# A decoder layer on one core: the product with values of each attention unit, split into two halves of 256 queries with score tiles between them

## The chip, the cores and the metric

One core of one Trainium2 chip. The metric is the device time of one launch in microseconds; three runs of a kernel are made and the median counts. TensorE (PE), VectorE (DVE), ScalarE (ACT), GpSimd (POOL) and SyncE (SP) each run their own instruction list in order and wait on semaphores that the others raise.

## What is computed

A decoder layer with two attentions and a feed-forward part, each behind a layer norm and added to its input. x is 4 x 1024 x 256 in float32, 16 heads of 16 columns.

```python
x = x + _L0_attn_ref(_layernorm(x), W_qkv, b_qkv, W_out, b_out)
x = x + _L0_xattn_ref(_layernorm(x), ctx_1024, ctx_1024, Wq, bq, Wk, bk, Wv, bv, Wo, bo)
x = x + _L0_ffn_ref(_layernorm(x), W_fc, ln_w, ln_b, W_proj)
...
energy = jnp.einsum('bqhe,bkhe->bqhk', q, k)            # attention over 1024 keys
attn = jax.nn.softmax(energy, axis=-1) / sqrt(E)
out = jnp.einsum('bihv,bvhd->bihd', attn, v)
```

The change lies in the first attention alone: 4 batches x 16 heads x 1024 queries x 1024 keys.

## The kernel before

The kernel has three stages: projections to queries, keys and values (about the first 130 us), the attention over 1024 keys (to about 785 us), and cross attention with the feed-forward part (the rest). The change touches the second.

**Units.** The heads are taken in groups of four, so there are 16 groups of a batch and four heads. A group has two halves of 512 queries, and each half has eight blocks of 128 keys. One *unit* U (0 to 255) is one block of keys against one half of the queries for the four heads. `KB` is 8, `CH` is 512, `UNITS` is 16. For each unit TensorE does three kinds of work.

- `scores(U, k)` (L1543), k = 0 to 3: the transposed score tile of one head, 128 keys by 512 queries, in float32r. It goes to one of three PSUM banks in turn, so tile n waits until the exponential of tile n - 3 is done (`exp_done`).
- `values(U)` (L1556): four matmuls with 32 columns of values each, side by side in the four column groups of the array, in float32. They read the probabilities of the unit and add up in bank 4 over the eight units of a half. It waits until all four exponentials of the unit are done. The last unit's matmul stops the sum, ScalarE copies bank 4 to `ot`, and the first unit of the next half waits for that (`o_copied`).
- `max_tile(t)` (L1427): a score tile with the queries on the partitions, one of 32 for each half of a later group, from which VectorE takes the row maxima that the softmax subtracts. There are four for each unit. They go round four banks (3, 5, 6, 7), so one waits for VectorE's reduction of the tile four places earlier (`max_reduced`). The maxima are split in two parts, transposed by TensorE (`max_transpose`, L1527, once for every 32 tiles, ahead of the tile with t % 32 == 8), copied by ScalarE to `mt` (L711), and written by SP into the rows of the queries that the score tiles read (`m_loaded`).

A score tile contracts over 50 rows and a maximum tile over 48, in one of two strips of 64 partitions (0 to 63, or 64 to 127), by the head. Two neighbours on different strips run at once.

**Order.** It is written out by hand for each engine. TensorE's loop over U is the one the diff shows: a maximum tile, a score tile of the next unit, three times over, then the product with values, then the next unit's fourth score tile and the fourth maximum tile. After `LAST_ROWS` (243) there are no more maximum tiles and other work of the next stage comes in. ScalarE's order is

```python
            for U in range(GROUPS * UNITS):
                if U % KB == 4 and U // KB + 1 < HALVES - 1:
                    m_copy(U // KB + 1)
...
                if U + 1 < GROUPS * UNITS:
                    act.wait_ge(pv_done, U)
                    exps(U + 1, 0, 3)
...
                if U % KB == KB - 1:
                    act.wait_ge(pv_done, U + 1)
                    act.wait_ge(o_written, O_WRITES * (U // KB))
                    act.activation(ot[:], ps[:, 4, :], ACT.Copy).then_inc(o_copied, 1)
                if U + 1 < GROUPS * UNITS:
                    exps(U + 1, 3, 4)
```

The probabilities have two buffers, so the exponentials of unit U + 1 wait for the product of unit U - 1 (`pv_done`). `m_copy` waits for the transpose (`m_transposed`). In units 72, 74, 76 and 78 ScalarE also takes the absolute values of a piece of the feed-forward weights (L729). VectorE reduces the maximum tiles one after another (L1021).

Of the kernel before, what the change touches and what calls it, by code (L numbers as in the profile page):

```python
# [30 lines left out]
CH = 512  # L31
NCH = T // CH
# [8 lines left out]
GROUPS = B * NG  # L41
KB = S // P
QC = S // CH
UNITS = QC * KB
# [52 lines left out]
EARLY_TILES = 2 * EARLY_PAIRS * (NCH - EARLY)  # L97
LEAD = EARLY_TILES
LAST_ROWS = GROUPS * UNITS - 13
# [19 lines left out]
HALVES = 2 * GROUPS  # L119
# [32 lines left out]
def build(nc, x, ctxT, wqkv, bqk, bv, wout, bout, wqT, bq2, wkT, bk2, wvT, bv2, woT, bo2,  # L152
# [10 lines left out]
    with ctx:  # L163
        def sb(name, shape, dt=F32, where=ctx):
            return where.enter_context(nc.sbuf_tensor(name, shape, dt))
# [4 lines left out]
        ps = ctx.enter_context(nc.psum_tensor("ps", [P, 8, 512], F32))  # L170
# [48 lines left out]
        prob = sb("prob", [P, 2, 2, 2, CH], F32, ab)  # L219
        Qs = [sb(f"Qs{i}", [P, HG // STRIPS, S], F32, ab) for i in range(NG)]  # L220
        Ks = [sb(f"Ks{i}", [P, HG // STRIPS, S], F32, ab) for i in range(NG)]
        V_all = sb("V_all", [P, V_ALL + D], F32, ab)
# [65 lines left out]
        parts_ready = sem("parts_ready")  # L288
# [6 lines left out]
        max_reduced = sem("max_reduced")  # L295
# [7 lines left out]
        pv_done = sem("pv_done")  # L303
# [1082 lines left out]
        def _(pe):  # L1386
# [125 lines left out]
            def max_tile(t):  # L1512

                if t >= TILES:
                    return
                if t % HALF == 8:
                    max_transpose(t // HALF - 1)
                if t % MAXT == 0:
                    b, g = divmod(t // MAXT, NG)
                    pe.wait_ge(group_loaded[g], GROUP_LOADS * (b + (g > 0)))  # L1520
                score_tile(max_bank("tile", t), t)

            def max_transpose(f):

                r = max_bank("rows", f)
                pe.wait_ge(m_split, f + 1)
                pe.transpose(ps[:, r, 0:P], msp[:], ident[:]).then_inc(m_transposed, 1)  # L1527

            def scores(U, k):

                group, s = divmod(U, UNITS)
                if group == NG * B:
                    return
                g, (qc, kb) = group % NG, divmod(s, KB)
                n, j = 4 * U + k, ST_HEADS[k]
                if kb == 0 and k == 0:
                    pe.wait_ge(m_loaded, 16 * HG * (U // KB + 1))
                if n in ST_BEFORE:
                    pe.wait_ge(exp_done, ST_BEFORE[n] + 1)
                elif n >= ST_TAIL:  # L1540
                    pe.wait_ge(max_reduced, TILES)
                    pe.wait_ge(m_copied, HALVES)
                pe.matmul(ps[:, ST_BANK[n], :], stack(Ks[g], j, ROWS, slice(kb * P, (kb + 1) * P)),  # L1543
                          stack(Qs[g], j, ROWS, slice(qc * CH, (qc + 1) * CH)), start=True, stop=True).then_inc(st_done, 1)

            def values(U):

                group, s = divmod(U, UNITS)
                b, g = divmod(group, NG)
                kb = s % KB  # L1550
                pe.wait_ge(exp_done, 4 * U + 4)
                if kb == 0 and U:
                    pe.wait_ge(o_copied, U // KB)
                for j in range(HG):
                    v = ((b * KB + kb) * H + g * HG + j) * VCOL
                    i = pe.matmul(ps[32 * j:32 * j + 32, 4, :], V_all[:, v:v + 32],  # L1556
                                  prob[:, U % 2, j // 2, j % 2, :], start=(kb == 0), stop=(kb == KB - 1))
                i.then_inc(pv_done, 1)

            freed = {"t2": (t2_copied, 2), "q2": (q2_copied, 2), "s": (less_done, 8), "pt": (pt_copied, 8), "val": (o2_copied, 2),  # L1560
                     "o2": (x2_added, 2), "out": (x1_added, 2), "t3": (t3_low, 2)}
# [49 lines left out]
            def q2(c, m):  # L1611
                if not 0 <= c < NCH:
                    return
                pe.wait_ge(t2_copied, 2 * c + 2)
                r = x_bank("q2", c, m)
                for k in range(KT):
                    n = mm(ps[:, r, :], w_q2[:, k, m * P:(m + 1) * P], xn2T[:, k, :], k, KT)
                n.then_inc(q2_done, 1)
# [2 lines left out]
            scores(0, 3)  # L1621
            for U in range(GROUPS * UNITS):
                t = LEAD + 4 * U
                if U == LAST_ROWS:
                    max_transpose(HALVES - 1)
                max_tile(t)
                scores(U + 1, 0)
                max_tile(t + 1)
                scores(U + 1, 1)
                if U == 0:  # L1630
                    pe.wait_ge(max_reduced, EARLY_TILES)
                max_tile(t + 2)
                scores(U + 1, 2)
                if U == 0:
                    pe.wait_ge(parts_ready, 4 * NCH)
                if U > LAST_ROWS:
                    scores(U + 1, 3)
                if U == GROUPS * UNITS - 1:
                    q2(0, 0)
                values(U)  # L1640
                if LAST_ROWS < U <= LAST_ROWS + 3:
                    prepare(U - LAST_ROWS - 1)
                if TAIL_OUT <= U < TAIL_OUT + 2:
                    out_proj(0, U - TAIL_OUT)
                if U == TAIL_T2:
                    t2(0, 0)
                    t2(0, 1)
                if U <= LAST_ROWS:
                    scores(U + 1, 3)
                max_tile(t + 3)  # L1650


            pe.wait_ge(exp_done, EXPS)
            def x_scores(c, t):
# [229 lines left out]
```

## Time and profile before

| | |
|---|---|
| median of three runs | 1169.06 us (1167.9 to 1171.06) |
| the profiled execution | 1169.54 us, its span 1167.6 us |
| PE busy | 1133.1 us, 97% |
| DVE busy | 992.8 us, 85% |
| ACT busy | 856.8 us, 73% |
| attention stage, 130 to 785 us | PE 651.54, DVE 616.33, ACT 535.53 us busy of 655.00 |
| granted TensorE clock in that stage | 1.00 |

The busy time of PE counts the time in which a matmul is anywhere between its start and its modelled end, so two starts may lie further apart than the work needs and PE still reads as busy. What an engine needs is read from starts that follow one another without a wait. A timeline row merges neighbours of one kind: its first number is the start of the first, its second the time from there to the end of the last, and xN is their count. A float32 matmul makes two records of weight load and matmul (so the product with values of a unit is x8), a float32r one makes one.

### The profile page before, as it was taken

How to read it: one execution, taken by the hardware profiler on the slowest of the kernel's cores; microseconds unless marked ns; L12 is line 12 of the kernel's file. 1: busy time of each engine (PE TensorE's matmuls, PEld its weight loads, DVE VectorE, ACT ScalarE, POOL GpSimd, SP SyncE). 2: the span in 40 equal slices, each digit the busy share in tenths (PEclk: the TensorE clock that was granted, in tenths of full speed). 3: DMA queues.
4: the chain of work that ended last, by engine and by line, in shares of the span. 5: the costliest groups of instructions: out<-in, count | busy, mean ns of one | idle time of the engine just before them, and what ended most of it. 6: DMA issues, size and time to landing. Idle time of an engine off the chain costs nothing.

```text
span 1167.6 us, 19014 instructions
## 1 busy us (share of the span) xinstructions
PE 1133.1 (97%) x6664; PEld 597.5 (51%) x6664; DVE 992.8 (85%) x1863; ACT 856.8 (73%) x1606; POOL 303.9 (26%) x469
## 2 busy tenths in 40 slices
PE   8999999999999999999999999999899999999986
PEld 6544333333333333333333333344568778778776
DVE  5678899999999999999999999976768778878844
ACT  4312588888888888888888888876468877788874
POOL 2124010220220220220121000012665656565532
PEclk9999999999999999999999999999899999999998
DMA  5878113562321330340341300023301220200001
GB/s 180 267 217 234 75 21 51 112 138 31 62 47 23 65 60 7 66 60 14 58 61 33 45 7 11 7 67 83 89 26 33 76 70 4 73 19 19 1 19 37
DMA packets 45918, 74.98 MB, mean 64 GB/s; under 512 B 10112, under 2 KB 23808, under 8 KB 45824
## 3 DMA queue, kind: packets, MB, share of 16 engines
q1 hardware_dynamic: 36176, 46.50, 13.7%
q0 software_dynamic: 9648, 27.27, 13.6%
q8 instruction: 53, 0.87, 0.3%
q14 instruction: 41, 0.34, 0.1%
HBM read 47.53 MB, written 25.69 MB: 63 GB/s over the span
## 4 chain that ended last, share of the span: by engine, by line
PE 88%; DVE 5%; ACT 4%; issue 1%; DMA 1%; SPq 1%; POOL 0%; DVEq 0%; ACTq 0%; POOLq 0%
PE ps L1543 22%; PE ps L1556 22%; PE ps L1388 18%; PE ps L1427 10%; PE ps L1746 5%; PE ps L1664 2%; PE ps L1733 2%; PE ps L1676 2%; ACT ot L781 1%; ACT prob L718 1%; PE ps L1687 1%; PE ps L1593 1%; DVE maxes L1014 1%; DMA Ks<-qk_scratch 1%; PE ps L1527 1%
## 5 line engine op out<-in xcount | busy, mean ns | idle before, releaser
L1021 DVE TENSOR_REDUCE maxes<-ps 128x1 f32<-128x512 f32 x968 | 606.8, 683 | 31.7 <-PE ps L1427 15.4
L718 ACT ACTIVATE prob<-ps 128x512 f32<-128x512 f32 x1024 | 531.8, 603 | 119.2 <-PE ps L1543 117.7
L1543 PE MATMUL ps<-Qs,Ks 50*128 50x512 f32 x1024 | 377.0, 452 | 4.3 <-ACT prob L718 2.0
L1543 PEld LDWEIGHTS ps<-Qs,Ks 50*128 50x128 f32 x1024 | 168.3, 185 | 309.8 <-ACT prob L718 298.3
L1427 PE MATMUL ps<-Ks,Qs 48*128 48x512 f32 x1024 | 322.1, 432 | 3.0 <-DVE maxes L1014 2.6
L1556 PE MATMUL ps<-prob,V_all 128*32 128x512 f32 x2048 | 273.6, 606 | 0.0
L1427 PEld LDWEIGHTS ps<-Ks,Qs 48*128 48x128 f32 x1024 | 166.8, 186 | 50.5 <-DVE maxes L1014 15.9
L378 POOL DMA_DIRECT2D Qs<-qk_scratch x90 | 44.5, 502 | 466.5 <-PE ps L1556 466.3
L606 POOL TENSOR_TENSOR pe_<-pe_,rsum 128x512 f32<-128x512 f32 x64 | 68.4, 1076 | 78.1 <-DVE rsum L1232 78.1
L1746 PE MATMUL ps<-t_p,fT 128*128 128x256 f32 x512 | 77.1, 297 | 2.4 <-DVE fT L1271 2.4
L1204 DVE TENSOR_REDUCE nmx<-ps 128x8 f32<-128x512 f32 x64 | 43.6, 681 | 39.9 <-PE ps L1664 39.9
L1556 PEld LDWEIGHTS ps<-prob,V_all 128*32 128x32 f32 x2048 | 40.3, 108 | 63.6 <-ACT prob L718 43.6
L1746 PEld LDWEIGHTS ps<-t_p,fT 128*128 128x128 f32 x512 | 66.8, 191 | 11.0 <-issue 7.3
L705 ACT ACTIVATE parts<-ps,b_qk 128x512 fp32r<-128x512 f32 x32 | 22.0, 688 | 68.0 <-PE ps L1388 68.0
L1388 PE MATMUL ps<-t_fc,xn3T 128*128 128x512 f32 x256 | 68.3, 409 | 0.2 <-DVE xn3T L1263 0.2
L1271 DVE SCALAR_TENSOR_TENSOR fT<-ps,ln_w,fT 128x512 fp32r<-128x512 f32 x64 | 46.9, 740 | 19.3 <-ACT fT L885 19.2
L1388 PE MATMUL ps<-xnT_a,w_qkv 128*128 128x512 f32 x128 | 61.3, 612 | 0.0
L885 ACT ACTIVATE fT<-ps,ln_w 128x512 fp32r<-128x512 f32 x64 | 43.5, 687 | 21.7 <-PE ps L1733 20.2
L1388 PEld LDWEIGHTS ps<-t_fc,xn3T 128*128 128x128 f32 x256 | 46.3, 188 | 14.5 <-issue 5.7
L562 POOL TENSOR_TENSOR x_b<-x_in,b_out 128x1024 f32<-128x1024 f32 x8 | 18.9, 2362 | 128.9 <-DMA x_in<-in_x 128.9
L806 ACT ACTIVATE pT<-ps 128x512 f32<-128x512 f32 x64 | 36.5, 595 | 21.3 <-PE ps L1676 21.2
L1223 DVE TENSOR_REDUCE psum<-pe_ 128x8 f32<-128x512 f32 x64 | 42.7, 668 | 6.9 <-ACT pe_ L797 6.7
(153 smaller groups left out, 1276.2 us busy)
## 6 DMA issues: line engine op xcount, KB each, us to landing
qk_scratch<-parts SPq DMA_DIRECT2D x32, 512.0 KB, 5.2
Qs<-qk_scratch POOLq DMA_DIRECT2D x90, 128.0 KB, 5.2
Ks<-qk_scratch POOLq DMA_DIRECT2D x90, 128.0 KB, 7.5
o_scratch<-ot SPq DMA_DIRECT2D x128, 32.0 KB
x_in<-in_x SPq DMA_DIRECT2D x8, 512.0 KB, 7.0
on_raw<-o_scratch SPq DMA_DIRECT2D x8, 512.0 KB
r_raw<-r_scratch SPq DMA_DIRECT2D x16, 256.0 KB
out<-xo SPq DMA_DIRECT2D x8, 512.0 KB, 2.9
```

Source lines behind the costliest of these rows:

```text
L378: queue.dma_start(dst[lo:lo + D, :, :], heads[r]).then_inc(loaded[g], 16)
L606: pool.tensor_tensor(p, p, rsum[:, i, :, None].broadcast_to([P, 8, CTX]), ALU.mult).then_inc(p_ready, 1)
L718: act.activation(prob[:, U % 2, j // 2, j % 2, :], ps[:, ST_BANK[n], :], ACT.Exp).then_inc(exp_done, 1)
L885: act.activation(fT[:, place, 0, :].bitcast(F32R), ps[:, r, :], ACT.Identity, scale=ln_w[:, t:t + 1]).then_inc(fh_ready, 1)
L1021: dve.tensor_reduce(maxes[:, qc, j * BLK + blk, half:half + 1], ps[:, MAX_BANK["tile", t], :], AX.X, ALU.max).then_inc(max_reduced, 1)
L1204: dve.tensor_reduce(nmx[:, i, :], ps[:, BANK["s", c, i], :].rearrange("p (h t) -> p h t", h=8), AX.X, ALU.max, negate=True).then_inc(nmx_d ...
L1271: dve.scalar_tensor_tensor(out=fT[:, place, 1, :].bitcast(F32R), in0=ps[:, r, :], scalar=ln_w[:, t:t + 1], in1=fT[:, place, 0, :], op0=ALU ...
L1388: return pe.matmul(o, lhsT, rhs, start=(k == 0), stop=(k == n - 1), **kw)
L1427: pe.matmul(ps[:, bank, :], stack(Qs[g], j, STACK, slice(q0, q0 + P)), stack(Ks[g], j, STACK, slice(half * 512, (half + 1) * 512)), start= ...
L1543: pe.matmul(ps[:, ST_BANK[n], :], stack(Ks[g], j, ROWS, slice(kb * P, (kb + 1) * P)), stack(Qs[g], j, ROWS, slice(qc * CH, (qc + 1) * CH)) ...
L1556: i = pe.matmul(ps[32 * j:32 * j + 32, 4, :], V_all[:, v:v + 32], prob[:, U % 2, j // 2, j % 2, :], start=(kb == 0), stop=(kb == KB - 1))
L1746: i = pe.matmul(ps[:, 6 + blk // 2, (blk % 2) * E:(blk % 2 + 1) * E], fT[:, ft_bank(c, t)[1], part, blk * P:(blk + 1) * P].bitcast(F32R), ...
```

## The change

TensorE's order in the units up to 243, and the shape of the product with values. The product of a unit is done in two halves, queries 0 to 255 and 256 to 511, each of four matmuls; only the unit that ends a half of the queries (U % 8 == 7) keeps it whole. Between the halves stand three of the four maximum tiles, score tiles 2 and 3 of the next unit, and score tile 0 of the unit after that; behind the second half stand the fourth maximum tile and score tile 1 of the unit after next. The sum in bank 4 starts with the first half of the first unit and ends with the second half of the last. No other engine's order changes.

```diff
-            def values(U):
+            def values(U, lo=0, hi=CH):
...
-                if kb == 0 and U:
+                if kb == 0 and lo == 0 and U:
                     pe.wait_ge(o_copied, U // KB)
                 for j in range(HG):
                     v = ((b * KB + kb) * H + g * HG + j) * VCOL
-                    i = pe.matmul(ps[32 * j:32 * j + 32, 4, :], V_all[:, v:v + 32],
-                                  prob[:, U % 2, j // 2, j % 2, :], start=(kb == 0), stop=(kb == KB - 1))
-                i.then_inc(pv_done, 1)
+                    i = pe.matmul(ps[32 * j:32 * j + 32, 4, lo:hi], V_all[:, v:v + 32], prob[:, U % 2, j // 2, j % 2, lo:hi],
+                                  start=(kb == 0 and lo == 0), stop=(kb == KB - 1 and hi == CH), skip_group_check=True)
+                if hi == CH:
+                    i.then_inc(pv_done, 1)
...
-                if U == LAST_ROWS:
-                    max_transpose(HALVES - 1)
-                max_tile(t)
-                scores(U + 1, 0)
-                max_tile(t + 1)
-                scores(U + 1, 1)
-                if U == 0:
-                    pe.wait_ge(max_reduced, EARLY_TILES)
-                max_tile(t + 2)
-                scores(U + 1, 2)
...
-                values(U)
+                if U <= LAST_ROWS:
...
+                    if U % KB == KB - 1:
+                        values(U)
+                    else:
+                        values(U, 0, CH // 2)
+                    if U:
+                        max_tile(t)
+                        max_tile(t + 1)
+                        max_tile(t + 2)
+                    scores(U + 1, 2)
+                    scores(U + 1, 3)
+                    scores(U + 2, 0)
+                    if U % KB < KB - 1:
+                        values(U, CH // 2, CH)
+                    max_tile(t + 3)
+                    scores(U + 2, 1)
+                else:
+                    for k in range(2 if U == LAST_ROWS + 1 else 0, 4):
+                        scores(U + 1, k)
+                    if U == GROUPS * UNITS - 1:
+                        q2(0, 0)
+                    values(U)
...
-                if U <= LAST_ROWS:
-                    scores(U + 1, 3)
-                max_tile(t + 3)
```

TensorE, units 3 and 4 before: the end of unit 3 (its product is the x3 row of line 1556), then unit 4, which has the transpose of the maxima. L1543 is a score tile, L1427 a maximum tile, L1556 values, L1527 the transpose.

```order
L1556 MATMUL ps<-prob,V_all 32x512 x3
L1543 MATMUL ps<-Qs0,Ks0 128x512 [waits exp_done]
L1427 MATMUL ps<-Ks1,Qs1 128x512 [waits max_reduced]
L1527 MATMUL ps<-ident,msp 128x128 [waits m_split,max_reduced]
L1427 MATMUL ps<-Ks1,Qs1 128x512 [waits max_reduced]
L1543 MATMUL ps<-Qs0,Ks0 128x512 [waits exp_done]
L1427 MATMUL ps<-Ks1,Qs1 128x512 [waits max_reduced]
L1543 MATMUL ps<-Qs0,Ks0 128x512 [waits exp_done]
L1427 MATMUL ps<-Ks1,Qs1 128x512 [waits max_reduced]
L1543 MATMUL ps<-Qs0,Ks0 128x512 [waits exp_done]
L1556 MATMUL ps<-prob,V_all 32x512 [waits exp_done]
L1556 MATMUL ps<-prob,V_all 32x512 x3
```

The same place now, from the end of unit 3 (last pair) to unit 4's second half and last pair.

```order
L1543 MATMUL ps<-Qs0,Ks0 128x512 [waits exp_done]
L1556 MATMUL ps<-prob,V_all 32x256 [waits exp_done]
L1556 MATMUL ps<-prob,V_all 32x256 x3
L1527 MATMUL ps<-ident,msp 128x128 [waits m_split,max_reduced]
L1427 MATMUL ps<-Ks1,Qs1 128x512 [waits max_reduced] x3
L1543 MATMUL ps<-Qs0,Ks0 128x512 [waits exp_done] x3
L1556 MATMUL ps<-prob,V_all 32x256 [waits exp_done]
L1556 MATMUL ps<-prob,V_all 32x256 x3
L1427 MATMUL ps<-Ks1,Qs1 128x512 [waits m_copied]
L1543 MATMUL ps<-Qs0,Ks0 128x512 [waits exp_done]
```

The transpose stood ahead of the whole product and now stands behind its first half. The three score tiles in the middle are tiles 2 and 3 of unit 5 and tile 0 of unit 6. An ordinary unit is the same without the transpose.

TensorE at unit 7, the last of its half, and the start of unit 8 now.

```order
L1556 MATMUL ps<-prob,V_all 32x512 [waits exp_done]
L1556 MATMUL ps<-prob,V_all 32x512 x3
L1427 MATMUL ps<-Ks1,Qs1 128x512 [waits max_reduced] x3
L1543 MATMUL ps<-Qs0,Ks0 128x512 [waits exp_done] x3
L1427 MATMUL ps<-Ks1,Qs1 128x512 [waits max_reduced]
L1543 MATMUL ps<-Qs0,Ks0 128x512 [waits exp_done]
L1556 MATMUL ps<-prob,V_all 32x256 [waits o_copied,exp_done]
L1556 MATMUL ps<-prob,V_all 32x256 x3
```

The whole product is followed by all eight tiles; before, three score tiles of the next unit stood ahead of it and the fourth behind.

## Rows read from the trace of the kernel before

**Rows 1.** The page: busy time by engine; the group of VectorE's reductions.

```profile
PE 1133.1 (97%) x6664; PEld 597.5 (51%) x6664; DVE 992.8 (85%) x1863; ACT 856.8 (73%) x1606; POOL 303.9 (26%) x469
...
L1021 DVE TENSOR_REDUCE maxes<-ps 128x1 f32<-128x512 f32 x968 | 606.8, 683 | 31.7 <-PE ps L1427 15.4
```

**Rows 2.** Waits, 300 to 700 us: who waited for whom, us, times, longest.

```profile
PEld ps L1543 <- ACT prob L718: 183.5, 290, 1.0
ACT prob L718 <- PE ps L1543: 66.7, 129, 0.6
```

**Rows 3.** Timeline, two ordinary units: start us, us, engine, line, operation.

```profile
609.24 1.06 PE L1556 MATMUL ps<-prob,V_all 128*32 128x512 f32 x8
...
612.84 0.49 PE L1543 MATMUL ps<-Qs,Ks 50*128 50x512 f32 x1
...
613.18 0.62 PE L1543 MATMUL ps<-Qs,Ks 50*128 50x512 f32 x2
...
613.37 2.07 ACT L718 ACTIVATE prob<-ps 128x512 f32<-128x512 f32 x4 [0.54 <-PE ps L1543]
...
613.42 0.61 PE L1427 MATMUL ps<-Ks,Qs 48*128 48x512 f32 x2
...
614.02 0.50 PE L1543 MATMUL ps<-Qs,Ks 50*128 50x512 f32 x1
...
614.45 1.06 PE L1556 MATMUL ps<-prob,V_all 128*32 128x512 f32 x8
```

**Rows 4.** Timeline, the unit that ends a half.

```profile
615.45 0.50 PE L1543 MATMUL ps<-Qs,Ks 50*128 50x512 f32 x1
...
615.58 0.60 ACT L781 ACTIVATE ot<-ps 128x512 f32<-128x512 f32 x1
...
616.08 2.06 ACT L718 ACTIVATE prob<-ps 128x512 f32<-128x512 f32 x4
...
617.15 1.06 PE L1556 MATMUL ps<-prob,V_all 128*32 128x512 f32 x8
```

**Rows 5.** Timeline, PE, near the stage's end: streamed score tiles, then a product.

```profile
782.30 0.73 PE L1543 MATMUL ps<-Qs,Ks 50*128 50x512 f32 x4
782.96 1.06 PE L1556 MATMUL ps<-prob,V_all 128*32 128x512 f32 x8
```

**Rows 6.** Timeline, DVE, 608.9 to 610.1 us.

```profile
608.80 1.87 DVE L1021 TENSOR_REDUCE maxes<-ps 128x1 f32<-128x512 f32 x3
```

**Rows 7.** Timeline, the unit with the transpose of the maxima.

```profile
603.89 1.07 PE L1556 MATMUL ps<-prob,V_all 128*32 128x512 f32 x8
...
605.32 0.33 PE L1527 MATMUL ps<-ident,msp 128*128 128x128 f32 x1
...
605.91 0.25 ACT L711 ACTIVATE mt<-ps 32x128 fp32r<-32x128 f32 x1
...
606.21 1.57 ACT L718 ACTIVATE prob<-ps 128x512 f32<-128x512 f32 x3
...
606.63 1.07 PE L1556 MATMUL ps<-prob,V_all 128*32 128x512 f32 x8
```

**Rows 8.** Groups by form, 0 to 170 us: float32 matmuls; busy us, mean ns.

```profile
L1388 PE MATMUL ps<-xnT_a,w_qkv 128*128 128x512 f32 x128 | 61.3, 612 | 0.0
L1388 PE MATMUL ps<-w_qkv,xnT_a 128*128 128x256 f32 x128 | 31.7, 391 | 4.6 <-DMA Ks<-qk_scratch 3.4 <-ACT xnT_a L699 0.8 <-ACT mt L711 0.4
```

**Rows 9.** Timelines of ACT and PE, a unit with an absolute-value pass.

```profile
319.97 1.06 ACT L729 ACTIVATE kbd<-w_fc 128x1024 f32<-128x1024 f32 x1
...
321.01 3.52 ACT L718 ACTIVATE prob<-ps 128x512 f32<-128x512 f32 x7
...
320.56 1.07 PE L1556 MATMUL ps<-prob,V_all 128*32 128x512 f32 x8
...
323.54 1.05 PE L1556 MATMUL ps<-prob,V_all 128*32 128x512 f32 x5
```

**Rows 10.** Timeline, PE, last stage: transposes in a stream.

```profile
1099.07 1.04 PE L1593 MATMUL ps<-ident,xn 128*128 128x128 f32 x8
```

More of the change, by code:

```diff
@@ L1623, in _ @@
                 t = LEAD + 4 * U
-                if U == LAST_ROWS:
-                    max_transpose(HALVES - 1)
-                max_tile(t)
-                scores(U + 1, 0)
-                max_tile(t + 1)
-                scores(U + 1, 1)
-                if U == 0:
-                    pe.wait_ge(max_reduced, EARLY_TILES)
-                max_tile(t + 2)
-                scores(U + 1, 2)
-                if U == 0:
-                    pe.wait_ge(parts_ready, 4 * NCH)
-                if U > LAST_ROWS:
-                    scores(U + 1, 3)
-                if U == GROUPS * UNITS - 1:
-                    q2(0, 0)
-                values(U)
+                if U <= LAST_ROWS:
+                    if U == LAST_ROWS:
+                        max_transpose(HALVES - 1)
+                    if U == 0:
+                        max_tile(t)
+                        scores(1, 0)
+                        max_tile(t + 1)
+                        scores(1, 1)
+                        pe.wait_ge(max_reduced, EARLY_TILES)
+                        max_tile(t + 2)
+                        pe.wait_ge(parts_ready, 4 * NCH)
+                    if U % KB == KB - 1:
[3 more added lines that the diff above has]
+                    if U:
+                        max_tile(t)
+                        max_tile(t + 1)
+                        max_tile(t + 2)
+                    scores(U + 1, 2)
+                    scores(U + 1, 3)
+                    scores(U + 2, 0)
[9 more added lines that the diff above has]
+                    values(U)
                 if LAST_ROWS < U <= LAST_ROWS + 3:
```

## The prediction

> **What bounds the kernel now.** I read the page first, then the stage in question by its waits, then one stretch of it instruction by instruction. The page says PE 97% busy [rows 1], which reads like a TensorE bound. The view of waits over 300 to 700 us corrects this [rows 2]: TensorE's weight loads for score tiles wait 183.5 us for ScalarE's exponentials, and ScalarE waits 66.7 us for score tiles. Two engines that both wait for each other form a loop, and the timeline gives its links [rows 3]. A unit begins where its product with values starts (609.24, two units later 614.45: 2.605 us each). The last score tile of the next unit follows it (612.84), its exponential starts 0.53 us later (613.37), a score tile that reuses the bank starts 0.65 us after that (614.02), the next product 0.43 us later (614.45), and it holds TensorE for 1.00 us (to 615.45 [rows 4]). 0.53 + 0.65 + 0.43 + 1.00 = 2.61: the whole period is this chain. TensorE's own work is less. From 612.84 the pairs of tiles on opposite row strips start 0.34 and then 0.24 us apart (613.18, 613.42); 1.00 + 0.34 + 0.24 + 0.24 and 0.33 from a streamed pair into a product (782.30 + 0.73 - 0.39 = 782.64 to 782.96 [rows 5]) give 2.15, so 0.46 us of each unit is stall. VectorE needs 4 reductions; one lasts 0.68 us and the next starts (1.87 - 0.68) / 2 = 0.60 us after it [rows 1, 6], so 2.40. ScalarE needs 4 exponentials of (2.07 - 0.60) / 3 = 0.49 us [rows 3], 1.95.
>
> Two units in every eight are longer. The one that ends a half of the queries has ScalarE's copy to ot between its exponentials: 614.45 to 617.15, 2.70 us [rows 3, 4]. The one with the transpose of the maxima has the copy to mt in front of them: 603.89 to 606.63, 2.74 us [rows 7]. So eight units take 6 x 2.605 + 2.70 + 2.74 = 21.07 us.
>
> **The change in an ordinary unit.** Call the start of the first half of the product 0. The product is two passes of four matmuls in each of which columns set the length; 512 against 256 columns in float32 differ by 612 - 391 = 221 ns [rows 8], so each pass is about 0.22 us shorter and a half takes 1.00 - 0.44 = 0.56 us. The bounds of this: 0.50 (exactly half of 1.00), and 0.70 if the fixed part were kept twice and each switch cost another 0.1. Then TensorE runs three pairs: two maximum tiles at 0.56, a maximum tile with score tile 2 at 0.90, score tile 3 with tile 0 of the unit after at 1.14. The second half starts at 1.47, the last pair at 2.03, and the next first half 0.43 later (a pair fresh after a product, as 614.02 to 614.45): **2.46 us** of own work, 0.31 more than the 2.15 of before. The added cost is the second entry and exit of the product.
>
> The Trainium skill (TensorEngine Tiling (Array Packing), Key Properties) says that changing the tiling mode drains TensorE, which speaks against a change that doubles these switches. The trace agrees: 0.33 us into a product against 0.24 between pairs.
>
> The chain of waits is now another: score tile 2 starts at 0.90, its exponential 0.44 later (a streamed tile's record is 0.1 shorter than the 0.5 of a fresh one, so 0.53 less 0.09), the fourth exponential 0.485 after it, and 0.65 later it releases the next first half: 0.56 + 0.34 + 0.44 + 0.485 + 0.65 = **2.475 us**. It is just over TensorE's 2.46 and over VectorE's 2.40, so 2.475 is the period and 0.13 us a unit is gained. The cover is thin: three limits lie within 0.08 us. The score tiles in the middle don't stall: tile 0 of unit U+2 (1.14) waits for the second exponential, which starts at 0.32 and releases it at 0.97.
>
> **The unit with the transpose.** Before, the transpose stood ahead of the product and ScalarE's copy to mt was ready when ScalarE came to it: 605.32, copied at 605.91, next exponential at 606.21, 0.30 later [rows 7]. Now it stands behind the first half, which itself waits for the fourth exponential. ScalarE's order is unchanged: right behind that exponential it waits for the transpose. So: transpose at 0.56, copy at 0.56 + 0.33 + 0.03 = 0.92, first exponential of the next unit at 1.22 where an ordinary unit has it at -0.165, the second at 1.705. Tile 0 of unit U+2 needs the second: 1.705 + 0.65 = 2.355. It is in front of the second half in TensorE's order, which starts at 2.785; the last pair at 3.345, the next product at 3.345 + 0.43 = **3.775 us**, against 2.74 before. Queued behind the stalled tile are the second half, a maximum tile and a score tile; VectorE loses nothing that counts, since it has over a microsecond to spare in this unit.
>
> **The unit that ends a half.** Its product stays whole, but score tiles 2 and 3 of the next unit now come behind it; before, tile 2 came ahead, so that its exponential ran under the product. ScalarE's copy to ot stands between the exponentials of tiles 2 and 3. Chain: product 1.00, a pair 0.34, to the exponential 0.44, to the copy 0.485, to the fourth exponential 616.08 - 615.58 = 0.50, release 0.65 = **3.41 us**, against 2.70 before.
>
> **The rest.** Eight units: 6 x 2.475 + 3.775 + 3.41 = 22.04 us, 0.97 more than 21.07. There are 30 such eights in the 244 units that the change reorders (+29.0), and 4 ordinary units over (-0.5). In four units ScalarE also takes an absolute-value pass, which shifts the exponentials by 321.01 - 319.97 = 1.04 us; before, such a unit took 323.54 - 320.56 = 2.98, 0.375 over an ordinary one [rows 9]. By the same chain it takes now (0.875 for the first exponential, 2.01 for tile 0, 2.44 for the second half, 3.00, 3.43) 0.955 over one: +2.3. The m rows for the next half have from the copy at 605.91 + 0.25 to the first score tile that reads them some 7.0 us now and 3.775 + 2.475 + 1.14 - 1.17 = 6.2 after; no wait on them shows before, and I cost this at nothing. If their loads took longer than 6.2, each half would lose the excess. What comes before and behind the 244 units keeps its order and costs nothing. POOL's loads and SP's writes keep their place. Sum: +29.0 - 0.5 + 2.3 = **+30.8 us**. The profiled execution took 1169.54 us (0.5 over the median of the three, 1169.06): 1169.5 + 30.8 = **1200 us**, 2.6% slower.
>
> With a half at 0.50 an ordinary unit takes 2.415 and the transposing one 3.655: 21.56 for eight, 1187 us. With 0.70 TensorE's own work sets 2.46 + 2 x 0.14 = 2.74: 23.9 for eight, 1255 us; I take the low value since [rows 8] measure the difference itself.
>
> **Rivals.**
> (1) The copies don't hold. If ScalarE's two copies cost the new order no more than the old one, eight units take 6 x 2.475 + 2.70 + 2.74 = 20.29, which is 0.78 less: 1169.5 - 23.4 + 2 = 1148 us, **faster**. It decides at the point where the two long units together take less than 21.07 - 14.85 = 6.22 us; I get 7.19. For it: VectorE's four banks hold work over a short gap, and the normal unit is quicker. Against: VectorE is not what the chain waits for, and both copies stand in a strictly ordered queue between exponentials [rows 4, 7]. Chance 0.06.
> (2) TensorE can't issue fast enough. A float32 product is two records for each matmul, so a unit goes from 16 to 24 pairs of weight load and matmul. The densest long stream in the trace is transposes, (1.04 - 0.27) / 7 = 0.11 us each [rows 10]; 24 x 0.11 = 2.64 us a unit. That gives 6 x 0.165 x 30 = 30 us more: 1230 us. For: no stretch of the trace goes faster for long. Against: those transposes each load 128 columns of weights, values load 32. Chance 0.10.
> The Trainium skill (TensorE: Matmul & The Clock Gate, Wait — 56ns, not 53.3ns?) puts the sequencer at about 62 ns for a matmul without hardware decode; 24 of these would be 1.5 us, no bound, unless the loads cost as much again (an estimate of 3.0 us). No run here shows which.
> (3) The two effects cancel: the ordinary unit at 2.40 and the long ones 0.3 us shorter than worked out give 21.0 for eight, no change. Chance 0.04.
>
> **How the numbers follow.** My forecast, 1200, has 0.80. Within 0.3% (3.5 us, about what a measurement of this kernel can tell from no change) lies rival 3, 0.04. Faster is rival 1, 0.06. Slower is the rest, 0.90. The range leaves out rival 1 and the highest part of rival 2 and of the long half: low end the half at 0.50 less 0.2 us in the two long units of each eight, 1187 - 6 = 1181; high end 1230.
>
> **What would show it.** Starts of products in the profile after: ordinary units 2.4 to 2.5 apart, one of eight 3.8 with ScalarE idle ahead of the mt copy (a wait for the transpose, about 1.1 us, absent before), one of eight 3.4 with ScalarE idle ahead of the third exponential. A half should take 0.56 us, and the weight loads of score tiles should wait less for ScalarE in ordinary units. I am wrong if ScalarE doesn't wait for the transpose, or if ordinary units take over 2.6 us (rival 2 or a dearer half, told apart by whether the gap stands inside the products or between them).

## The result, and the profile after

| | before | changed |
|---|---|---|
| median of four runs | 1169.42 us | 1211.16 us (1204.31 to 1222.83) |
| ratio to before | | 1.034, 95% interval 1.029 to 1.038 |
| the profiled execution | 1169.54 us | 1211.86 us, span 1209.9 us |

3.4% slower, where 2.6% (1200 us) was forecast. Ratios here and below leave out executions over 1.5% above the fastest of their kernel; with a single core these are the ones in which TensorE's clock stayed low longest, of which more below.

The page of the changed kernel, with the lines that answer to [rows 1], ScalarE's exponentials and the granted clock (tenths of full speed, 40 slices of the span):

```profile
PE 1156.3 (96%) x8376; PEld 620.2 (51%) x8376; DVE 994.2 (82%) x1863; ACT 857.0 (71%) x1606; POOL 303.9 (25%) x469
...
PEclk9999999999959999999999999999999999999998
...
L1021 DVE TENSOR_REDUCE maxes<-ps 128x1 f32<-128x512 f32 x968 | 608.7, 683 | 74.2 <-PE ps L1427 70.7
L718 ACT ACTIVATE prob<-ps 128x512 f32<-128x512 f32 x1024 | 534.5, 599 | 134.9 <-PE ps L1543 125.1
```

VectorE and ScalarE do the same work as before (994 and 857 us), in a span 42 us longer. VectorE's idle time ahead of its reductions went from 31.7 to 74.2 us: it is starved more than before. TensorE again reads 96% busy, which says as little as before. The 5 in the clock's row is new.

The view of waits of the changed kernel, 410 to 810 us, as long a window as that of [rows 2] (columns as there):

```profile
PEld ps L1427 <- DVE maxes L1021: 84.4, 194, 0.8
...
PEld ps L1556 <- ACT prob L718: 49.1, 144, 0.8
...
PEld ps L1543 <- ACT prob L718: 22.5, 54, 0.7
ACT mt L711 <- PE ps L1527: 17.8, 18, 1.0
```

A line of the view of [rows 2] that answers to the first of these:

```profile
PEld ps L1427 <- DVE maxes L1021: 6.1, 19, 0.3
```

Score tiles wait far less for exponentials (22.5 us in 400 instead of 183.5), products wait more (49.1 us instead of 27.0), and ScalarE's copy to mt now waits for the transpose, 1.0 us each time. That wait was absent before. The line that grew most, TensorE's weight loads waiting for VectorE (6.1 to 84.4 us), is not what it seems. Most of it is the weight loader's idle time behind a half of a product, 0.41 us each time:

```profile
438.15 0.64 PE L1556 MATMUL ps<-prob,V_all 128*32 128x256 f32 x8
438.72 0.32 PEld L1427 LDWEIGHTS ps<-Ks,Qs 48*128 48x128 f32 x3 [0.41 <-issue]
...
439.63 0.64 PE L1556 MATMUL ps<-prob,V_all 128*32 128x256 f32 x8
440.20 0.18 PEld L1427 LDWEIGHTS ps<-Ks,Qs 48*128 48x128 f32 x1 [0.41 <-DVE maxes L1021]
```

The next tile comes 0.57 us after the start of the half in both places, whether the view names VectorE or nobody, so VectorE costs nothing there.

Timeline of the changed kernel, the unit with the transpose and the ordinary one behind it (columns as in [rows 7]):

```profile
440.66 0.64 PE L1556 MATMUL ps<-prob,V_all 128*32 128x256 f32 x8
441.23 0.33 PE L1527 MATMUL ps<-ident,msp 128*128 128x128 f32 x1
...
441.60 0.27 ACT L711 ACTIVATE mt<-ps 32x128 fp32r<-32x128 f32 x1 [0.99 <-PE ps L1527]
441.78 2.01 ACT L718 ACTIVATE prob<-ps 128x512 f32<-128x512 f32 x4
...
442.88 0.18 PEld L1543 LDWEIGHTS ps<-Qs,Ks 50*128 50x128 f32 x1 [0.30 <-ACT prob L718]
443.31 0.64 PE L1556 MATMUL ps<-prob,V_all 128*32 128x256 f32 x8
...
444.31 0.64 PE L1556 MATMUL ps<-prob,V_all 128*32 128x256 f32 x8
444.88 0.73 PE L1427 MATMUL ps<-Ks,Qs 48*128 48x512 f32 x3
445.22 0.63 PE L1543 MATMUL ps<-Qs,Ks 50*128 50x512 f32 x3
445.78 0.64 PE L1556 MATMUL ps<-prob,V_all 128*32 128x256 f32 x8
...
446.81 0.64 PE L1556 MATMUL ps<-prob,V_all 128*32 128x256 f32 x8
```

Counted from 440.66: transpose at 0.57, copy at 0.94 after ScalarE had idled 0.99, the third score tile (tile 0 of the unit after next) only at 2.22, second half at 2.65, next product at 3.65. The ordinary unit: 444.31 to 446.81, 2.50 us; a half is followed by the next tile after 0.57 us.

And the unit that ends a half, whole product and all tiles behind it (compare [rows 4]):

```profile
449.33 1.06 PE L1556 MATMUL ps<-prob,V_all 128*32 128x512 f32 x8
...
451.13 0.60 ACT L718 ACTIVATE prob<-ps 128x512 f32<-128x512 f32 x1 [0.87 <-PE ps L1543]
451.62 0.59 ACT L781 ACTIVATE ot<-ps 128x512 f32<-128x512 f32 x1
...
452.10 1.58 ACT L718 ACTIVATE prob<-ps 128x512 f32<-128x512 f32 x3
452.75 0.16 PEld L1556 LDWEIGHTS ps<-prob,V_all 128*32 128x32 f32 x8 [0.79 <-ACT prob L718]
```

3.42 us from product to product, with ScalarE idle 0.87 us for tile 2. (This whole product is also what ends the sum in bank 4, not a second half.) Eight units take 6 x 2.505 + 3.64 + 3.42 = 22.09 us; read from the starts of the products, 26 of the 30 eights lie within 0.03 us of that, three others between 21.8 and 22.8. One is far off, units 72 to 79, at 37.1 us. The windows of the changed kernel around it (busy us and count by engine, granted clock, DMA share, GB/s):

```profile
300.00:330.00 30.00, 28.34 (x235) 11.39 (x237) 27.01 (x47) 23.82 (x48) 5.89 (x12) 0.98 0.42 63
330.00:345.00 15.00, 15.00 (x87) 5.17 (x90) 8.44 (x17) 7.80 (x15) 0.00 (x0) 0.50 0.01 2
...
365.00:400.00 35.00, 34.27 (x298) 14.07 (x298) 32.08 (x57) 27.17 (x55) 2.73 (x6) 1.00 0.30 44
```

From 329.1 to 363.2 us TensorE's clock was granted at half, the lower of its two levels (1.2 GHz for 2.4). An ordinary unit takes 4.32 us there. The stretch begins in unit 72, which is the first with an absolute-value pass and also comes right behind a unit that ends a half. In the stage before no such stretch is seen after the one of 3.4 us at 129.8.

### The profile page after: what moved, and what is told of

It is laid out like the page before. It is cut to its first block, busy times and chain, and to the rows that moved or that the text cites. A ratio compares the mean times of both kernels' runs of the same rounds, so it can differ in the third digit from the quotient of the medians.

```text
span 1209.9 us, 22438 instructions
## 1 busy us (share of the span) xinstructions
PE 1156.3 (96%) x8376; PEld 620.2 (51%) x8376; DVE 994.2 (82%) x1863; ACT 857.0 (71%) x1606; POOL 303.9 (25%) x469
## 4 chain that ended last, share of the span: by engine, by line
PE 87%; DVE 4%; ACT 4%; issue 2%; DMA 1%; SPq 1%; POOL 0%; DVEq 0%; ACTq 0%; POOLq 0%
PE ps L1556 25%; PE ps L1427 22%; PE ps L1388 18%; PE ps L1543 8%; PE ps L1758 5%; PE ps L1676 2%; PE ps L1745 2%; PE ps L1688 2%; ACT ot L781 1%; ACT prob L718 1%; PE ps L1699 1%; PE ps L1594 1%; DVE maxes L1014 1%; DMA Ks<-qk_scratch 1%; PE ps L1527 1%
## 5 line engine op out<-in xcount | busy, mean ns | idle before, releaser
L1021 DVE TENSOR_REDUCE maxes<-ps 128x1 f32<-128x512 f32 x968 | 608.7, 683 | 74.2 <-PE ps L1427 70.7
L1556 PE MATMUL ps<-prob,V_all 128*32 128x256 f32 (+1 forms) x3760 | 324.8, 418 | 14.5 <-ACT prob L718 14.5
L1543 PE MATMUL ps<-Qs,Ks 50*128 50x512 f32 x1024 | 318.0, 438 | 9.0 <-ACT prob L718 8.9
L1427 PE MATMUL ps<-Ks,Qs 48*128 48x512 f32 x1024 | 320.0, 479 | 2.8 <-DVE maxes L1014 2.6
L1427 PEld LDWEIGHTS ps<-Ks,Qs 48*128 48x128 f32 x1024 | 126.3, 187 | 224.8 <-DVE maxes L1021 144.0
L1543 PEld LDWEIGHTS ps<-Qs,Ks 50*128 50x128 f32 x1024 | 160.2, 188 | 60.2 <-ACT prob L718 47.7
L1556 PEld LDWEIGHTS ps<-prob,V_all 128*32 128x32 f32 x3760 | 74.5, 109 | 153.7 <-ACT prob L718 82.0
L1388 PE MATMUL ps<-t_fc,xn3T 128*128 128x512 f32 x256 | 68.3, 409 | 0.2 <-DVE xn3T L1263 0.2
```

The source lines that it names most:

```text
L1021: dve.tensor_reduce(maxes[:, qc, j * BLK + blk, half:half + 1], ps[:, MAX_BANK["tile", t], :], AX.X, ALU.max).then_inc(max_reduced, 1)
L1388: return pe.matmul(o, lhsT, rhs, start=(k == 0), stop=(k == n - 1), **kw)
L1427: pe.matmul(ps[:, bank, :], stack(Qs[g], j, STACK, slice(q0, q0 + P)), stack(Ks[g], j, STACK, slice(half * 512, (half + 1) * 512)), start= ...
L1556: i = pe.matmul(ps[32 * j:32 * j + 32, 4, lo:hi], V_all[:, v:v + 32], prob[:, U % 2, j // 2, j % 2, lo:hi], start=(kb == 0 and lo == 0), s ...
```

## Experiments

My theory: the two ScalarE copies make two long units of each eight, and this outweighs a real gain in the ordinary unit. The rival: the halves, with their switches and their extra instructions, cost the time. The last three runs ask where the clock falls. The runs were made on three chips, each time with the kernel before beside them, whose median was 1166.6 to 1166.8 us there. Unit lengths are medians of the differences between the starts of products in the profiled execution. U % 8 = 4 is the transposing unit, U % 8 = 7 the one that ends a half.

### The transpose ahead of its unit

```diff
                     if U % KB < KB - 1:
                         values(U, CH // 2, CH)
+                    if (t + 4) % HALF == 8 and t + 4 < TILES:
+                        max_transpose((t + 4) // HALF - 1)
                     max_tile(t + 3)
```

(and `max_tile` no longer issues it.)

> The changed kernel with the transpose of the maxima issued right behind the second half of the unit before, ahead of the last pair, instead of behind the first half of its own unit. Theory (ScalarE, in order, waits for the transpose with the next unit's exponentials behind it): the unit with the transpose falls from 3.64 to about 2.5 us, the one before it grows from 2.51 to about 2.75, so about 26 us less than the changed kernel's 1211: 1185. Rival (the halves and the extra switches are the cost, the long unit only shows them): the transposing unit stays over 3.3 us and the time within 5 us of 1211.

1190.41 us, ratio 1.018 (1.014 to 1.022), the lowest run 1182.8. The unit fell from 3.64 to 2.76 and the one before it grew to 2.73; eight units 21.43 instead of 22.09, 20 us in all. The rival is out. The unit did not reach 2.5, for a reason I had not seen. Timeline of this run:

```profile
429.54 0.27 ACT L711 ACTIVATE mt<-ps 32x128 fp32r<-32x128 f32 x1
...
429.86 0.64 PE L1554 MATMUL ps<-prob,V_all 128*32 128x256 f32 x8
...
430.43 0.97 PE L1427 MATMUL ps<-Ks,Qs 48*128 48x512 f32 x3
430.91 0.18 PEld L1427 LDWEIGHTS ps<-Ks,Qs 48*128 48x128 f32 x1 [0.29 <-DVE maxes L1021]
430.91 0.73 PE L1541 MATMUL ps<-Qs,Ks 50*128 50x512 f32 x3
431.47 1.09 ACT L718 ACTIVATE prob<-ps 128x512 f32<-128x512 f32 x2 [0.71 <-PE ps L1541]
```

The copy no longer waits. But the third maximum tile waits for VectorE (0.29 us), and score tile 2 stands behind it in TensorE's order (0.48 us after the first pair instead of 0.34), so that the chain over its exponential starts late.

### Score tile 2 ahead of the whole product

```diff
                     if U % KB == KB - 1:
+                        scores(U + 1, 2)
                         values(U)
+                        max_tile(t)
+                        max_tile(t + 1)
+                        scores(U + 1, 3)
+                        scores(U + 2, 0)
+                        max_tile(t + 2)
```

The other units keep the changed order.

> The changed kernel with score tile 2 of the next unit ahead of the whole product in the unit that ends a half, and tiles 3 and 0 ahead of the third maximum tile. Theory (in that unit the exponential of tile 2 no longer runs under the product, and the copy to ot adds itself between it and tile 3's): the unit before grows from 2.5 to 2.93 us, this one falls from 3.42 to 2.42, 0.57 less in eight units, 17 us: 1194. Rival (o_copied alone sets it, which the tile order does not change): stays within 3 us of 1211.

1207.51 us, ratio 1.031 (1.025 to 1.037). The time alone decides nothing: it is 3.7 us under the changed kernel's, close to the rival's 3, and the profiled execution has a stretch of 34.1 us at half the clock in its first units. The units decide. Two came out at 2.93 and 2.42 as worked out, but the first unit of the next half grew from 2.51 to 2.76. Eight units 21.78, 0.31 less instead of 0.57, which is 9 us of the 17. So `o_copied` is not what sets this unit, but nearly half the gain is lost again in the next one.

### Both together

> Both moves of the two runs before together. Theory: eight units take 4 x 2.505 + 2.75 + 2.505 + 2.93 + 2.42 = 20.6 us against 22.1 changed and 21.07 before: 1158 us with TensorE's clock at full speed in the stage, 1169 if its stretch at 0.5 stays. So the ordinary unit's gain of 0.10 us is real and this is faster than the kernel before. Rival (halves and switches cost time by themselves): not faster than 1169.

1172.93 us, ratio 1.006 (1.002 to 1.011): eight units 21.10 us, which is the 21.07 of before again. Both long units are gone and the gain of the ordinary ones is just eaten by two that stay at 2.76. The timeline shows the wait for VectorE in the transposing unit as above, and the same 0.30 us stand in the first unit of a half (457.36 us):

```profile
425.64 0.18 PEld L1427 LDWEIGHTS ps<-Ks,Qs 48*128 48x128 f32 x1 [0.30 <-DVE maxes L1021]
```

The forecast of 1158 had these two units at 2.505: 2 x 0.25 x 30 = 15 us, the whole of its error.

### Halves with nothing between them

```diff
-                values(U)
+                if U <= LAST_ROWS:
+                    values(U, 0, CH // 2)
+                    values(U, CH // 2, CH)
+                else:
+                    values(U)
```

in the kernel before, with the new `values`.

> The kernel before with one edit: the product with values of units up to 243 is done in two halves of 256 queries one right after the other, with nothing between them; the order is otherwise that of before. Theory (a half costs its columns, and what the split adds is the entry and exit around it): the product's records run on in one block of about 1.0 to 1.05 us, the unit stays 2.61 to 2.65, and the time is 1167 to 1180. Rival (more and shorter matmuls cost issue time or let the clock fall by themselves): the unit grows by 0.1 us or more, over 1192, or stretches at 0.5 of the clock appear in the stage as in the changed kernel.

1170.65 us, ratio 1.0023 (1.0008 to 1.0039). The product goes on for 1.01 us in 16 records where it took 1.00 in 8:

```profile
420.00 1.07 PE L1556 MATMUL ps<-prob,V_all 128*32 128x256 f32 x16
421.01 0.50 PE L1543 MATMUL ps<-Qs,Ks 50*128 50x512 f32 x1
```

The extra instructions cost 0.01 us a product and 0.04 us in eight units (21.12 against 21.08), about 1 us of the 3.8 between the medians; the profiled execution, at 1167.2 us the quickest of the ten, does not show the rest. No stretch at half the clock shows in the stage of this profile. With tiles between them two halves take 2 x 0.57 us instead of 1.01, so what the split adds is the second entry and exit.

### The product whole in the new order

```diff
-                    if U % KB == KB - 1:
-                        values(U)
-                    else:
-                        values(U, 0, CH // 2)
+                    values(U)
...
-                    if U % KB < KB - 1:
-                        values(U, CH // 2, CH)
```

> The changed kernel with every unit's product whole at the place of its first half; the order of the tiles is the changed one. Theory (the chain product, tile 2, its exponential, the next exponential, next product): an ordinary unit is 1.00 + 0.34 + 0.45 + 0.49 + 0.65 = 2.93 us instead of 2.51, the unit that ends a half 3.42, the one with the transpose about 3.9 or less; eight units about 24.9, so 84 us over the changed kernel: 1295. Rival (the halves are what costs, the new order of tiles is what gains): the unit is 2.5 or less and the time under 1211.

1277.45 us, ratio 1.097 (1.091 to 1.103). Ordinary units take 2.93 us, the one that ends a half 3.42, the one with the transpose 3.60. The timeline of an ordinary unit:

```profile
631.39 1.06 PE L1556 MATMUL ps<-prob,V_all 128*32 128x512 f32 x8
632.39 0.72 PE L1427 MATMUL ps<-Ks,Qs 48*128 48x512 f32 x3
632.73 0.62 PE L1543 MATMUL ps<-Qs,Ks 50*128 50x512 f32 x3
...
633.84 0.49 PE L1543 MATMUL ps<-Qs,Ks 50*128 50x512 f32 x1 [0.24 <-ACT prob L718]
634.32 1.07 PE L1556 MATMUL ps<-prob,V_all 128*32 128x512 f32 x8
```

This is the chain with 1.00 in place of 0.57. The new order of tiles alone is a loss of 0.33 us a unit against before, since tile 2's exponential no longer runs under the product; the halves give 0.43 back. They are what gains in this change. It also splits the 3.42 us of the unit that ends a half: 2.93 is what any whole product costs in this order, so of the 0.92 us over an ordinary unit 0.43 come from leaving the product whole, and 0.49 from the copy to ot. The total came out 18 us under the 1295: 9 from the transposing unit, 3.60 instead of 3.9; the rest fits the long stretch at half the clock, which the 1211 contains and this profile does not have.

### Score tiles 2 and 3 right behind the first maximum tile

```diff
                         if U:
                             max_tile(t)
-                            max_tile(t + 1)
-                            max_tile(t + 2)
                         scores(U + 1, 2)
                         scores(U + 1, 3)
+                        if U:
+                            max_tile(t + 1)
+                            max_tile(t + 2)
                         scores(U + 2, 0)
```

on top of both moves above.

> The kernel of the run both_first with score tiles 2 and 3 right behind the first maximum tile, and the second and third maximum tile behind them. In both_first two units of eight stood at 2.76 us because the third maximum tile waited for VectorE with score tile 2 behind it, and the ordinary ones at 2.51 because of the chain over tile 2's exponential. Theory: both fall to TensorE's own work, 2.46 to 2.50, the sixth unit 2.7; eight units about 20.3 instead of 21.1, so 24 us less than both_first's 1173: 1150, about 1.5% faster than the kernel before. Rival (TensorE's own work or its issue already sets 2.51): the ordinary unit stays at 2.51, eight units 20.6 or more and the time 1158 or more. If stretches at 0.5 of the clock come, each of 30 us costs some 12 us on top.

1158.38 us (1150.23 to 1181.4), ratio 0.991 (0.988 to 0.994): **faster than before**, by less than 1%. Ordinary units take 2.47 us, the one before the last 2.70, the last 2.42, the transposing one 2.53, but the one ahead of it 2.93, since the transpose there now waits for VectorE's reduction of a tile:

```profile
457.68 0.64 PE L1554 MATMUL ps<-prob,V_all 128*32 128x256 f32 x8
458.46 0.14 PEld L1525 LDWEIGHTS ps<-ident,msp 128*128 128x128 f32 x1 [0.62 <-DVE maxes L1021]
```

Eight units 20.49 against the 20.3 worked out. The time is over the 1158 of the rival, but its mechanism, an ordinary unit held at 2.51, is out; what is missing is the 0.19 us in eight units (6 us) and the clock. Six of the twelve executions took 1150.2 to 1155.3 us at a mean clock of 0.990 to 0.995, the other six 1161.5 to 1181.4 at 0.964 to 0.983. The mean of all twelve, 1161.7 us, is 0.5% under the 1167.4 of the kernel before. The ordinary unit here is TensorE's own work at last, 0.57 + 0.34 + 0.23 + 0.32 to the second half, then 0.57 + 0.43:

```profile
430.77 0.64 PE L1554 MATMUL ps<-prob,V_all 128*32 128x256 f32 x8
431.34 0.50 PE L1427 MATMUL ps<-Ks,Qs 48*128 48x512 f32 x1
...
431.68 0.62 PE L1427 MATMUL ps<-Ks,Qs 48*128 48x512 f32 x2
431.92 0.39 PE L1541 MATMUL ps<-Qs,Ks 50*128 50x512 f32 x1
432.23 0.64 PE L1554 MATMUL ps<-prob,V_all 128*32 128x256 f32 x8
...
433.23 0.64 PE L1554 MATMUL ps<-prob,V_all 128*32 128x256 f32 x8
```

### ScalarE's copy to mt moved, and nothing else

```diff
-                if U % KB == 4 and U // KB + 1 < HALVES - 1:
-                    m_copy(U // KB + 1)
...
                     exps(U + 1, 0, 3)
+                if U % KB == 4 and U // KB + 1 < HALVES - 1:
+                    m_copy(U // KB + 1)
```

> The changed kernel with one edit on ScalarE and none on TensorE: the copy to mt stands behind the exponentials of tiles 0 to 2 of the next unit instead of ahead of them. Theory (the transposing unit is long because ScalarE waits for the transpose with the exponentials behind it): tile 2 starts at 0.57 + 0.26 + 0.34 = 1.17 after the first half, its exponential at 1.62, the copy at 2.11, the fourth exponential at 2.41, the next product at 3.06, so the unit falls from 3.64 to about 3.06 and the time by 17 us, 1194 to 1196 plus what the clock adds. Rival (the transpose itself, a whole-array matmul behind a half, holds TensorE): it stays over 3.5 us.

1197.01 us, ratio 1.019 (1.016 to 1.023), the two lowest 1186.5 and 1187.7. The unit with the transpose falls from 3.64 to 3.12 without a change on TensorE (465.26 to 468.37), eight units from 22.09 to 21.57, and the copy no longer waits:

```profile
465.26 0.64 PE L1556 MATMUL ps<-prob,V_all 128*32 128x256 f32 x8
465.83 0.14 PEld L1527 LDWEIGHTS ps<-ident,msp 128*128 128x128 f32 x1 [0.41 <-issue]
...
467.10 0.60 ACT L718 ACTIVATE prob<-ps 128x512 f32<-128x512 f32 x1 [0.91 <-PE ps L1543]
...
467.59 0.25 ACT L711 ACTIVATE mt<-ps 32x128 fp32r<-32x128 f32 x1
...
468.37 0.64 PE L1556 MATMUL ps<-prob,V_all 128*32 128x256 f32 x8
```

The wait in ScalarE's order is worth 0.52 of the 1.13 us by which this unit was longer than an ordinary one. The other 0.61 stay: the transpose takes 0.26 on TensorE (465.83 to the next tile at 466.09), the copy 0.16 ahead of the fourth exponential (467.59 to 467.75), and most of the rest lies around score tile 2, whose exponential starts at 467.10, 1.84 after the first half where 1.62 was expected. That the transpose alone holds TensorE for over 3.5 us, the rival, is out.

### The same copy moved in the fastest version

> The kernel of tiles_2_3_early with the transpose back at the head of its own unit (behind the first half of the product) and the copy to mt on ScalarE moved behind the exponentials of tiles 0 to 2. Theory: the unit before the transpose falls from 2.93 to 2.48, the transposing one grows from 2.53 to 2.75 (the transpose adds 0.26 to TensorE's own work), eight units 20.25 instead of 20.49: 7 us less than tiles_2_3_early, 1151 against 1166.8 before, ratio 0.987. Rival (the copy that is late now delays the fourth exponential, or m3, which waits for it): the transposing unit is 3.0 or more and the time is not under 1158.

1155.13 us (1149.12 to 1167.4), ratio 0.987 (0.984 to 0.989). The unit ahead of the transpose fell to 2.47 as expected, but the transposing unit stands at 3.00 in most eights, not 2.75: the third maximum tile waits for VectorE again, with tile 0 beside it, 0.40 us behind the pair ahead of it instead of 0.24:

```profile
446.20 0.18 PEld L1427 LDWEIGHTS ps<-Ks,Qs 48*128 48x128 f32 x1 [0.41 <-DVE maxes L1021]
```

Eight units 20.49, no better than before this edit; the medians' 3 us are within the spread of either. The rival had the length of this unit right, but the time is under its 1158.

### Where the clock falls: the absolute-value passes

```diff
-                if U % 2 == 0 and 72 <= U < 80:
-                    abs_part(U // 2 - 36)
+                if U % 8 == 1 and 72 <= U < 104:
+                    abs_part(U // 8 - 9)
```

in the changed kernel:

> The changed kernel with ScalarE's four absolute-value passes in units 73, 81, 89 and 97 instead of 72, 74, 76 and 78. Theory on the part that the prediction did not have (a stretch of 34 us at 0.5 of the clock which begins in unit 72): the passes open stalls that let the clock fall, and close together they keep it down, so spread out there is no long stretch at 0.5 and the time is 11 us less, 1200. Rival (the clock falls by chance or by the transposing units alone): a stretch at 0.5 of some 30 us stays somewhere in the stage and the time is 1205 to 1220.

1213.63 us, ratio 1.037 (1.032 to 1.042). A unit with a pass takes 3.43, 0.93 over an ordinary one (0.955 was worked out), and the clock stays up in units 72 to 104; but a stretch of 30.7 us at half the clock stands at 664.7 us, in unit 192, so nothing is won. The rival held: the clock falls without a pass nearby. Unit 192, like 72, comes right behind a unit that ends a half.

The changed kernel as it is, once more:

> The changed kernel once more, on the chip of the three others, to see where its clock falls. Theory (the clock falls in stalls of the long units, at a place that shifts from run to run): stretches at 0.5 come again but not at the same place, 1204 to 1225 us. Rival (the absolute-value passes cause it): again in unit 72, and only there.

1212.15 us, ratio 1.038 (1.034 to 1.042). The stretch came at the same place, unit 72, from 330.5 us and for 44.4 us. Here my theory of a shifting place missed. It does not show that the passes make the clock fall: in the run with the passes spread it fell in unit 192, where there is none.

And the spread passes in the fastest version:

> copy_later_full with the four absolute-value passes in units 73, 81, 89 and 97. Theory on the clock (falls come where TensorE stalls longest, and passes close together give such stalls): fewer or shorter stretches at 0.5, spread of the runs smaller and the median 2 to 5 us under copy_later_full. Rival (the clock falls by chance elsewhere too): same median within 2 us and the same spread.

1152.05 us (1149.32 to 1152.46), ratio 0.986 (0.985 to 0.988), the best of all. No stretch over 6.8 us is in its profile, and all four runs have a mean clock of 0.993 or 0.994, where the five of the run before lie between 0.976 and 0.996. It is 3 us under that one's median. This fits the theory, but four runs against five, with stretches that come in some executions only, don't prove it, and 0.7 of the 3 us is the passes themselves (2.1 us in four eights instead of 2.8 in one).

## Why the prediction was right, and where it was off

- **The ordinary unit.** Forecast 2.475, measured 2.505. The step "a half is 0.56" held (0.57). Both the chain (0.57 + 0.34 + 0.46 + 0.49 + 0.65) and TensorE's own work are 2.51 here; five terms were each short by 0.00 to 0.02. 184 units x 0.03 = 5.5 us.
- **The unit with the transpose.** Forecast 3.775, measured 3.64: ScalarE goes on 0.18 us after the copy to mt starts, not the 0.30 read from the trace of before [rows 7]. There the score tile that the next exponential reads may have set it, since it started only 0.62 us before that exponential; this is not tested. 30 x 0.135 = 4 us the other way. ScalarE's wait for the transpose was worked out as about 1.1 us and measured as 0.99. The mechanism is shown twice, by moving the transpose and by moving the copy.
- **The unit that ends a half.** Forecast 3.41, measured 3.42, of two causes about equal in size (the whole product and the copy to ot), as the chain had them.
- **The rest of the sum.** Eight units 22.09 against 22.04: +1.5 us. The unit with an absolute-value pass, +0.93 against +0.955.
- **What was missing.** The stretch at half the clock. Units 72 to 79 took 37.1 us; 22.1 and four passes at 0.93 make 25.8, so it cost 11.3 us in the profiled execution. With it the forecast is 1200.3 + 1.5 + 11.3 = 1213, against 1211.9. From the first product of the stage to that of unit 244 the changed kernel takes 689.03 us against 645.66, 43.4 more where 30.8 were forecast; behind it both take 392.3. The prediction had no term for the clock: it took the 1.00 of the stage before as given, though the change opens stalls of about a microsecond in two units of eight. That the total still lies inside the range is in part luck: the upper end, 1230, came from rival 2 and not from a doubt about the clock.
- **Rival 1 (the copies don't hold)** is out for the changed kernel: its eights take 22.09 us and not 20.29. That later versions come near its 1148 (1149 in the lowest runs) doesn't speak for it, as they also place the score tiles otherwise.
- **Rival 2 (issue)** is out: 24 pairs of weight load and matmul fit in 2.47 us, 0.10 us each, and 16 records instead of 8 for one product cost 0.01 us. The 3.0 us that the prediction estimates behind this rival is out by the same number.
- **The drain at a mode switch** (the Trainium skill, TensorEngine Tiling (Array Packing), Key Properties) stands as the trace put it: 0.32 us into a half against 0.23 between pairs, and 0.10 more for the first pair behind one. It is paid twice a unit now. It does not decide against the split, since the cover was 0.46 us of stall.
- **Slips in the working.** The last step of the sum into a product is 782.64 to 782.96, 0.32 us and not 0.33. With the half at 0.50 the sum gives 1186 and not 1187 us, with 0.70 about 1257 and not 1255. None of these moves the forecast.
- **VectorE's waits** were costed at nothing and this was right for the changed kernel. In the transposing unit the third maximum tile does wait 0.24 us for a reduction, but the unit's chain runs over the copy and the exponentials behind it. VectorE's waits became the next limit as soon as the long units were mended, and cost 0.25 us in each of two units.

## What to carry to other kernels

When an order is changed on one engine, walk the whole period of the other engines' orders, not only the common step: the gain was 0.10 us in six steps of eight and the loss 0.9 and 0.7 us in the other two, where an in-order engine had a rare copy between its usual work and, in one of them, the product was left whole. Put what starts a long chain (here score tiles 2 and 3) ahead of what only feeds an engine with buffered work (here the maximum tiles), and place a rare copy behind the work that others wait for. The split itself paid in this order: 0.43 us a unit. With three such repairs the kernel is 1.3% faster than before, and 1.4% with the absolute-value passes spread as well. No run tried the repaired order with the product whole.

## What the runs showed of the hardware that was not expected

- TensorE's clock fell to half in the attention stage and stayed there for 23.9 to 68.3 us in 8 of the 10 profiled executions with product halves and tiles between them, though the engine was busy (33.28 of 34 us in the changed kernel) at 4.32 us a unit. With the halves adjacent the one profile has no such stretch (mean clock of the ten executions 0.991 to 0.995), with the product whole it has one of 6.8 us.
- What TensorE had done just before such a fall shows a pattern. Some falls stand in the first unit of the stage, at 131 to 133 us. Of the others in the stage most begin in the first unit of a half, units 16, 56, 72, 128, 160, 192 and 224 in one run or another: 11 of these 12 falls follow a unit of 3.42 us, in which ScalarE idles 0.87 us (451.13 in the changed kernel) and TensorE waits 0.24 and then 0.48 us for its exponentials. Where that unit takes 2.42 us (five runs), a fall stands there once, in unit 72, for 6.8 us. The remaining falls are in units 77 and 156. Against it stands the run with the product whole, which has the 3.42 us units and no fall behind one. So that the stalls of the unit that ends a half let the clock fall is a guess from the traces; no run tested it. Why the clock stays low so long in the one order and comes back after 3.4 us in the kernel before stays open: no run here changed that alone.
- Four matmuls of 32 columns side by side over 256 queries take 0.22 us a pass (420.25 to 420.46 us in the run with adjacent halves; 0.24 for the first), over 512 queries 0.45 (609.24 to 609.69 us before). They scale with the queries, and the fixed part of a product is about 0.1 us: 1.00 less two passes of 0.45.
